# Attention stage: the inverse roots of the layer norm by one GpSimd power, and ScalarE's two casts in the other order

## The reference

```
x = x + tanh(g_xattn[0]) * attention(layernorm(x), ctx, ctx)     # 8 heads over a width of 128
x = x + tanh(g_ffn[0])   * mixture0(layernorm(x))                # 8 experts, top 2
x = x + tanh(g_xattn[1]) * summary(layernorm(x), ctx)            # decayed sum of the context
x = x + tanh(g_ffn[1])   * mixture1(layernorm(x))                # 64 experts, top 4, and 2 shared ones

layernorm(x) = (x - mean(x)) / sqrt(var(x) + 1e-5)
attention: per head softmax(q k / 64^0.5 / 64^0.5) v
mixture0's router: the two largest of the 8 logits of layernorm(x) @ w_gate
```

## Time and profile before

| | us |
|---|---|
| median of three executions | 1229.34 |
| span of the profiled execution, first to last instruction | 1221.8 |
| PE busy in the span | 1070.8 (88%) |
| DVE busy | 706.4 (58%) |
| POOL busy | 600.0 (49%) |
| ACT busy | 494.6 (40%) |
| mean granted PE clock | 0.957 |

### The profile page before, as it was taken

How to read it: one execution, slowest core, us unless ns; L and a number is a source line. 1 busy time by engine, 2 the same in 40 slices (tenths; PEclk the granted TensorE clock), 3 DMA queues, 4 the chain that set the end, 5 groups by cost and what they waited for, 6 DMA issues and landing times. The chain is left out here.

```text
span 1221.8 us, 19314 instructions
## 1 busy us (share of the span) xinstructions
PE 1070.8 (88%) x5503; PEld 752.8 (62%) x5503; DVE 706.4 (58%) x1598; ACT 494.6 (40%) x874; POOL 600.0 (49%) x742
## 2 busy tenths in 40 slices
PE   3999989899856999999788989999997999999930
PEld 2555555555425777777358748677586777788720
DVE  4678888878524888888377616546231333343426
ACT  2565555655404888888433022212211222222200
POOL 5465555656433666666542555647250434343530
PEclk9999999999987999999899989999998999999975
DMA  9854356534165333333440212022025999899739
GB/s 309 298 193 142 135 191 226 183 117 153 63 212 180 100 108 104 103 104 102 168 152 6 78 55 83 26 80 75 5 67 207 365 347 312 279 309 352 199 73 365
DMA packets 115968, 202.39 MB, mean 166 GB/s; under 512 B 19847, under 2 KB 28039, under 8 KB 115898
## 3 DMA queue, kind: packets, MB, share of 16 engines
q1 hardware_dynamic: 95802, 167.47, 40.0%
q0 software_dynamic: 20096, 34.08, 10.0%
HBM read 133.36 MB, written 87.03 MB: 180 GB/s over the span
## 5 line engine op out<-in xcount | busy, mean ns | idle before, releaser
L1959 POOL DMA_INDIRECT sums<-summary,m_token x64 | 99.1, 1549 | 163.2 <-DMA sums<-summary,m_token 81.3
L973 POOL TENSOR_TENSOR m_down_lo<-wo,m_down_hi 128x512 fp32r<-128x512 f32 x80 | 133.3, 1686 | 80.7 <-ACT m_down_hi L1048 80.7
L491 PE MATMUL bank<-win,vT 128*128 128x512 f32 x256 | 124.1, 597 | 0.0
L661 DVE TENSOR_REDUCE negmax<-bank 128x1 bf16<-128x512 f32 x128 | 86.9, 679 | 38.8 <-PE bank L498 38.4
L584 ACT ACTIVATE win<-bank 128x512 f32<-128x512 f32 x128 | 69.4, 594 | 97.3 <-PE bank L483 95.1
L1062 DVE TENSOR_TENSOR m_up_lo<-w,m_up_hi 128x1024 fp32r<-128x1024 f32 x80 | 99.2, 1240 | 10.2 <-ACT m_up_hi L1035 8.4
L1272 POOL DMA_INDIRECT tab<-stage_up,slot x64 | 66.4, 1038 | 50.7 <-DVE slot L1607 32.5
L498 PE MATMUL bank<-k_hi,q_parts 128*128 128x512 f32 x128 | 70.8, 553 | 23.2 <-DVE q_parts L739 14.5
L1982 PE MATMUL bank<-y,m_w 128*128 128x128 f32 x736 | 89.7, 275 | 0.0
L1982 PEld LDWEIGHTS bank<-y,m_w 128*128 128x128 f32 x736 | 86.4, 193 | 0.5 <-issue 0.5
L2137 PE MATMUL bank<-w_sd,stage_gate 128*128 128x512 f32 x192 | 84.9, 598 | 0.3 <-DVE stage_gate L2127 0.3
(11 more groups left out here) (289 smaller groups left out, 2481.6 us busy)
## 6 DMA issues: line engine op xcount, KB each, us to landing
tab<-zeros SPq DMA_DIRECT2D x16, 1056.0 KB
m_w<-in_L_ffn_Wg SPq DMA_DIRECT2D x46, 256.0 KB
m_w<-in_L_ffn_Wu SPq DMA_DIRECT2D x46, 256.0 KB
m_w<-in_L_ffn_Wd SPq DMA_DIRECT2D x46, 256.0 KB
m_x<-tab SPq DMA_DIRECT2D x40, 256.0 KB, 2.6
ytab<-m_y SPq DMA_DIRECT2D x40, 256.0 KB, 2.0
stage_up<-tab SPq DMA_DIRECT2D x32, 264.0 KB
m_x<-tab SPq DMA_DIRECT2D x32, 264.0 KB
```

The source lines that it names most:

```text
L491: nc.tensor.matmul(pO[s * 2 + h][:], vT[:, s, sb_, h:h + 2, :].rearrange("p a c -> p (a c)"), probs[:, sb_ % 2, h, :], start=(sb_ == 0), s ...
L661: nc.vector.tensor_reduce(negmax[:, s, m:m + 1], pM[:], AX.X, ALU.max, negate=True).then_inc(pm_read, 1)
L973: nc.gpsimd.tensor_tensor(dn_lo[:, m, :], row(wo0, e * MB + m), dn_hi[:, m, :], ALU.subtract).then_inc(dn_lo_ready, 1)
L1959: nc.gpsimd.indirect_dma_start(T["sums1"][e % SUMS], bass.IndirectOffsetOnAxis(token[:, e % META:e % META + 1], 0), y[:, e % RING, :], Non ...
```

## The change

The three Newton rounds and the first guess go. DVE only computes var + eps and signals; POOL raises it to the power -0.5 in one operation, from a constant tile that it fills once at the start. ACT's two casts at the end of a step change places, each with its wait. The scratch tiles `half` and `nt` go, `power` comes, and two semaphores have new names.

```
@@ gpsimd, constants @@
             nc.gpsimd.memset(wsel[:], 0.0)
+            nc.gpsimd.memset(power[:], -0.5)
@@ gpsimd, step @@
                     a, z = cols[0], cols[-1] + 1
-                    pool.wait_ge(guess_ready, i + 4)
-                    for _ in range(3):
-                        newton(nc.gpsimd, pool, rstd[:, a:z], ve[:, a:z], nt[:, a:z])
+                    pool.wait_ge(var_ready, i + 4)
+                    nc.gpsimd.tensor_tensor(rstd[:, a:z], ve[:, a:z], power[:, a:z], ALU.pow)
+                    pool.drain()
...
-                    nc.gpsimd.engine_nop().then_inc(newton_done, 1)
+                    nc.gpsimd.engine_nop().then_inc(ln_done, 1)
@@ scalar, step @@
                         need(act, qk_done, i + 1)
+                        need(act, kd_loaded[s], 64 * u + 128)
+                        for h in range(2):
+                            last = nc.scalar.copy(k_hi[:, s, h, :], kd[:, s, h, :])
+                        last.then_inc(k_hi_ready, 1)
                         need(act, q_ready, i + 3)
                         for h in range(2):
                             hp = slice(HEAD * h, HEAD * h + HEAD)
                             last = nc.scalar.copy(q_parts[hp, s, h, :], q[hp, :])
                         last.then_inc(q_hi_ready, 1)
-                        need(act, kd_loaded[s], 64 * u + 128)
-                        for h in range(2):
-                            last = nc.scalar.copy(k_hi[:, s, h, :], kd[:, s, h, :])
-                        last.then_inc(k_hi_ready, 1)
@@ vector, step @@
-                        need(dve, newton_done, i + 3)
+                        need(dve, ln_done, i + 3)
...
-                        rsqrt_guess(nc, dve, rstd[:, a:z], mv[:, a:z, 1], half[:, a:z], ve[:, a:z]).then_inc(guess_ready, 1)
+                        nc.vector.tensor_scalar(ve[:, a:z], mv[:, a:z, 1], LN_EPS, None, ALU.add).then_inc(var_ready, 1)
```

More of the change, by code:

```diff
@@ L36 @@
 SUMS = 2
-RSQRT_MAGIC = float(0x5F3759DF)
 def seen(k):
@@ L239, in attention @@
         rstd = sb("rstd", [P, 2])
-        half, ve, nt = sb("half", [P, 2]), sb("ve", [P, 2]), sb("nt", [P, 2])
+        ve, power = sb("ve", [P, 2]), sb("power0", [P, 2])
         ln1 = sb("ln1", [P, 2, 2])
@@ L268, in attention @@
         q_hi_ready, q_split, recip_ready = sem("q_hi_ready"), sem("q_split"), sem("recip_ready")
-        guess_ready, ln2_ready, xn_ready = sem("guess_ready"), sem("ln2_ready"), sem("xn_ready")
+        var_ready, ln2_ready, xn_ready = sem("var_ready"), sem("ln2_ready"), sem("xn_ready")
         ctx_loaded = [sem(f"ctx_loaded_{n}") for n in range(4)]
-        ctx_used, newton_done = sem("ctx_used"), sem("newton_done")
+        ctx_used, ln_done = sem("ctx_used"), sem("ln_done")
         vT_full, vT_ready = sem("vT_full"), sem("vT_ready")
```

## The result

Measured side by side, twenty executions of each, the changed kernel takes 1231.91 us (1228.97 to 1235.64) and the kernel before 1226.96 us (1224.65 to 1232.51). The ratio is 1.0044 [1.0034, 1.0055]: slower by 5.4 us by the ratio and by 5.0 by the medians, with the whole interval on the slower side. I had forecast 4.7 us faster. The time is 0.9 us above the end of my range, and none of the rivals is what happened.

What follows compares the result with a forecast made beforehand. Bound: the attention stage's chain through five engines, with DVE's q split late, then 4.5 us behind the last maximum. Terms -2.3 - 0.4 + 0.9 - 0.4 - 2.5 = -4.7 us, from 1229.34 to 1224.6; range 1217 to 1231.

Steps and rivals of the forecast that it cites:

- The power: POOL's one-operation power in the attention stage: 0.7 us for two columns, 1.1 at the other end; neither counts in an inner step.
- the beginning: First attention steps up to step 0: an earlier first q split, no guess and a shorter later q split, taken as -2.3 us.
- the end: Step 15, before the weighted context: xn is ready earlier, so PE's transposes move from 332.3 to 329.8, -2.5 us.
- the wait for k's DMA: ACT's wait before the k cast, moved ahead of the q cast: k lands 1.8 us ahead of the cast, so no cost.
- Step 14: The attention step that has no k split: forecast to gain 0.4 us.
- The walk through `choose`: Inner steps: the earlier k split on POOL holds DVE's COPY and CAST in `choose`; 19.5 us a step, chance 0.45.
- R+15.0: Forecast start of the last maximum (m = 7), counted from R, the start of the inner step's first reciprocal.
- steps 2 to 13: +0.9: The twelve steps with both a k split and a `choose`: 12 of 19.5 us, 234.0 against 233.15 before.
- the q split's 2 us: DVE's q split in each inner step, alone once the k split is over earlier: 1.39 us instead of 3.43.
- The rival "slower": Small DVE operations hold POOL in return, k split about 3.2 us: 20.2 us a step, 1233 us in all, chance 0.13.
- 19.9 a step: Step length from which the rival "slower" was said to decide, with the last maximum (m = 7) at 121.2.

## Why the prediction was wrong, step by step

- **The power, the beginning, the end: right.** The power took 0.72 us (0.7). The start gained 2.7 us and the end 2.4, as forecast. In the inner steps the wait for k's DMA was covered. In the first 50 us it was not: ACT waited for `wout` 1.80 us before the k cast at 9.09 and 0.79 before that at 41.85, which it never did before the change. Step 14 gained 0.1 instead of 0.4.
- **The walk through `choose`: right.** COPY 0.89 (0.8), CAST 1.16 (about 1), last maximum R+15.05 (R+15.0), reciprocal R+19.57 (R+19.5). The Trainium skill (SBUF — State Buffer, Who interferes with whom) lists copies, casts and tensor_scalars among what GpSimd can block. I had no row for the COPY of two elements; the trace after is one, and it agrees.
- **The term "steps 2 to 13: +0.9": wrong, and it is the step that failed.** It set twelve steps at 19.5 each, with "maximum, negated maxima on PE, exponentials, values, copies" at 4.5 us throughout. It measured +14.7. Twelve of 19.56 would be 234.7, +1.6; the other 13.1 us are eight steps with TensorE at 1.2 GHz, 1.64 us each. Filling PE's idle stretch takes them away while the holds stay, and idle time alone brings them back. So the cause, PE's idle time ahead of the negated maxima, is shown from both sides.
- **How I missed it.** I placed the last maximum 1.4 us later and took the q split's 2 us away, and looked only at when the reciprocal comes. Both moves also shape PE's idle time: two short pieces became one long one. The granted clock was 1.00 from 50 to 335 us before, and I took that as given rather than as something that the schedule kept up. No rival named it. The rival "slower" had another mechanism (POOL held in return, the k split at 3.2 us); the k split took 2.50, so it is refuted; that its 1233 us lie near the measured time is chance.
- **What else was missing.** I compared only the order as changed with the order as it was. That the power alone, with the old order of the casts, would do better (−1.0%) was to be seen: the k split would have started behind the COPY and the CAST.

One sum of the rival "slower" is slightly off, without weight: twelve steps of 20.2 against 233.15 are +9.25, not +9.4. And the 19.9 a step "from which it decides" is where the total stays as it is; 0.2% slower needs 20.1.

What stays open, first: why eight of twelve steps had a fall. The idle times of the changed kernel don't sort them: 1.79 us before the halved stretch at 265.9, but 2.25 us before the full clock in the next step.

```profile
266.32 1.04 PE L448 MATMUL bank<-identb,negmax 128*128 128x128 bf16 x8 [1.79 <-DVE negmax L626]
287.29 0.62 PE L448 MATMUL bank<-identb,negmax 128*128 128x128 bf16 x8 [2.25 <-DVE negmax L626]
```

Over four of the kernels, by the idle time before the negated maxima of each step: of the 12 steps with 1.79 us or more after the change 8 had a fall, of the 13 with 1.67 or more in the kernel with the constant reductions 6, the one of 2.15 with the power alone, and none of its other steps (1.62 at most) or of those with the filling (0.94 at most).

Second: whether the one piece counts or the sum over the step. After the change both are larger than before, and no run cuts the 2 us into two pieces. Four steps speak for the one piece: two of the kernel with the constant reductions had a fall with 1.9 us of idle time in all, 1.67 and 1.69 of them in one piece, and two of the kernel before had none with 1.9 in three pieces of at most 1.1. That is too few to show it, since other steps with such a piece had no fall either.

## What to carry to other kernels

When an operation is moved, see not only which wait ends last but where the idle time of TensorE goes: with up to 1.9 us a step in pieces of at most 1.1 the full clock stayed here; with 2.0 to 2.3 us, nearly all in one piece, the clock fell in eight of twelve steps, at 1.6 us each on the critical chain. Look where a long GpSimd operation will land once its own cover is gone, and keep it off the short VectorE copies and casts: three other places for the same split were each worth about 1.5% against the one that the change gave it, 0.9% of it the clock. Two edits that are each harmless or good must be priced together.

## What the runs showed of the hardware

- After the change the granted clock fell to half within steps in which PE was never idle for more than 2.3 us at a time and was busy for 87 to 94% of each 50 us (43.4 to 46.9). Each time it stayed there for 3.4 us.
- Operations of two elements on DVE are held beside a long one of POOL nearly as long as the product of 128 x 16 in the earlier trace rows (1.09 us): the COPY took 896 ns at the median and the CAST 1156, against 148 and 168 at the least.
- The power costs POOL 0.55 to 0.58 us for one column of 128 and 0.71 to 0.73 for two; the one call that began beside a split of DVE (one column, at 13.80) took 1.06.

```profile
L384 POOL TENSOR_TENSOR rstd<-ve,power x20: 548/718/1058, 6.9 to 351.2; 128x2 f32<-128x2 f32 x12, 128x1 f32<-128x1 f32 x8
...
L639 DVE COPY top<-m x16: 148/896/965, 76.7 to 367.6; 128x2 f32<-128x2 f32 x8, 128x2 f32 x8
L641 DVE CAST idxf<-i x16: 168/1156/1171, 77.8 to 367.8; 128x2 f32<-128x2 uint32 x16
```
